# Decoder, second layer: weight loads behind a gather, one layernorm ahead of a softmax step, five weight folds moved into the self-attention

## The chip, the cores and the metric

One core of one Trainium2 chip runs the whole program in one launch. The metric is device time in microseconds (us), the median of several executions. TensorE (PE) multiplies and transposes, VectorE (DVE) and ScalarE (ACT) work on what it leaves in PSUM, GpSimd (POOL) works in SBUF, and SyncE (SP) issues nearly all the loads. Each engine takes its instructions strictly in the order written; semaphores order the engines among themselves.

## The reference

Two pre-norm decoder layers over x of 16 x 64 x 256 floats. The first is a Mamba block, a cross-attention and a routed feed-forward; the second is what the change touches:

```python
x = x + _L0_ffn_ref(_layernorm(x), w_router, w_fc, w_proj)      # two experts, top 1
x = x + _L1_attn_ref(_layernorm(x), Wqkv, b_qkv, Wout, b_out)   # 16 heads of 16, causal, bias by distance
x = x + _L1_xattn_ref(_layernorm(x), ctx, mask, Wq, Wk, Wv, Wo) # 16 heads of 128, 8 key/value heads
x = x + _L1_ffn_ref(_layernorm(x), w_gate, w_up, w_down)        # weights rounded to -1, 0, 1
```

In the second cross-attention the kernel never makes the keys or values: it multiplies Wv by Wo and Wq by Wk once per head ("folds"), and works with the context itself.

## The kernel before

The 1,024 tokens lie as 8 tiles of 128 rows (`x`, `xn`), in four groups g of two tiles. A layernorm of group g is `ln_add` (statistics, DVE), `ln_rstd` (ACT), `ln_scale` (DVE), `ln_turn` (PE transposes) and `ln_turned` (ACT copies to `xnT`). The batches fall into two halves of 512 tokens.

**Feed-forward of layer 0.** Ten sorted jobs; job s leaves its result by `result(s)` (ACT) and a store to `f_out` (SP). POOL's `gather(h)` (L487) fetches the rows of half h back into `xn` with four indirect DMAs, and DVE's `add_back(h)` (L1956) adds them to x. Before it, the same queue writes rows out by indirect DMAs (`scatter`, L485).

**Self-attention of layer 1.** Eight steps i, four heads of one half each; steps 0 to 3 are the first half, 4 to 7 the second. A step is `a_scores(i)` (PE, L1450), `a_shifts(i)` (DVE, L1999: add the bias L2004, row maximum L2008, subtract L2009), `a_exps(i)` (ACT, L828), `a_sums(i)` (DVE, L2015), `a_turn(i)` (PE, L1467), `a_turned(i)` (ACT, L835), `a_context(i)` (PE, L1480). Queries and keys come from `a_project(n)`, n = 0 to 3 for the first half, 4 to 7 for the second (L1426), and from `projected(n)` (ACT). All engines' orders are written out by hand: PE's in L1514 to L1584, ACT's in L851 to L908, DVE's in L2032 to L2096. On DVE the second half's `add_back(1)` and layernorm stand between steps 1 and 2, with `ln_scale(3, 2)` and `ln_scale(3, 3)` behind `a_shifts(2)`. On PE `a_scores(3)` stands ahead of `ln_turn(3, 2)`. On ACT, from step 5 on, `a_exps(i)` stands ahead of `a_turned(i - 1)`. `weight_sum(i)` (L844, ACT) takes the absolute sum of a feed-forward weight. `a_turn_rows` and `a_out` (PE) end a half, and `ln_add(4, g)` follows.

**Loads.** SP issues `wo1` (2,048 KB), `t_gate`, `t_up` and `t_down` (1,024 KB each) as soon as the feed-forward's last `hidden` and `down_rows` are done (L412 to L417).

**Cross-attention of layer 1.** `cross(1, ...)` (L1140 on PE, L664 on ACT) starts with 16 folds, 8 of `wvo` (L1158) and 8 of `wqk` (L1172). Each is one PSUM bank, banks 6 and 7 in turn, emptied by one ACT copy; the last `a_turn_rows(1)` and `a_out(1)` stand after the fourth and the eighth. Then come the first queries (L1184) and eight steps with the scores in L1231. `wvo` and `wqk` lie in region C, where the self-attention's queries, keys, values and softmax tiles lie as well, so no fold can be stored before these are done with.

POOL adds the output bias to all of x in one instruction (L503), and later rounds the three feed-forward weights in 36 instructions (L511 to L515).

## Time and profile before

| | before |
|---|---|
| median of 3 runs | 927.2 us (924.82 to 931.52) |
| the profiled execution | 926.82 us, of which the span of the profile is 924.9 us |
| mean granted clock of TensorE | 0.963 of full speed |
| self-attention, from the last job's result to the first query | 620.4 to 707.0 us of the span |
| cross-attention and feed-forward of layer 1, from the first query | 707.0 us to the end |

The profile is of one execution. All times within the kernel are us from the start of its span. Beside the span, 1.9 us of that execution lie outside it.

### The profile page before, as it was taken

The page shows a single profiled execution, that of the slowest core. Times are in us where ns is not written, and L with a number is a line of the kernel's source. Part 1 is how long each engine was busy: PE and PEld are TensorE (multiplying, and loading weights), DVE is VectorE, ACT ScalarE, POOL GpSimd, SP SyncE. Part 2 cuts the span into 40 slices and gives each one's busy share as a digit, 9 for nine tenths or more (in the row PEclk, how much of TensorE's full clock was granted, in tenths as well). Part 3 has the DMA queues.
Part 4 walks back from the last instruction along what each step waited for, and adds up shares of the span by engine and source line. Part 5 has one row for each costly group of instructions (what it writes and reads, how often), then busy time and mean ns, then how long its engine had stood idle before and what let it go on. Part 6 is the DMA issues. An engine that isn't in the chain of part 4 may idle for free.

```text
span 924.9 us, 12509 instructions
## 1 busy us (share of the span) xinstructions
PE 818.7 (89%) x5082; PEld 501.8 (54%) x5082; DVE 548.1 (59%) x666; ACT 434.1 (47%) x650; POOL 302.3 (33%) x147
## 2 busy tenths in 40 slices
PE   6687797977999889999999899997989799989976
PEld 2232333322445456566666676666677566667754
DVE  3799989899994232333433452437872534464686
ACT  3764666635524555555545312233554222232475
POOL 0089999899870000000001010102009990000000
PEclk9889999899999999999999999998989999999999
DMA  9666666776994100000000031415000000000001
GB/s 301 176 172 172 185 166 172 181 182 181 249 264 157 47 1 1 1 1 1 1 1 25 27 103 57 176 44 226 2 3 1 1 1 1 1 1 1 1 1 46
DMA packets 26377, 77.02 MB, mean 83 GB/s; under 512 B 3569, under 2 KB 10481, under 8 KB 25073
## 3 DMA queue, kind: packets, MB, share of 16 engines
q1 hardware_dynamic: 25552, 74.13, 27.8%
q0 software_dynamic: 768, 2.10, 0.6%
q8 instruction: 41, 0.67, 0.3%
q14 instruction: 16, 0.12, 0.0%
HBM read 68.75 MB, written 7.08 MB: 82 GB/s over the span
## 4 chain that ended last, share of the span: by engine, by line
PE 54%; DVE 13%; DMA 11%; ACT 10%; POOL 6%; issue 5%; SPq 0%; POOLq 0%; DVEq 0%; ACTq 0%
PE ps L1268 11%; PE ps L1184 9%; DMA region_b<-m_rows 5%; DMA region_c<-m_rows 4%; PE ps L1231 4%; PE ps L1367 4%; PE ps L1393 4%; POOL region_c L464 3%; PE ps L1256 3%; PE ps L1189 2%; POOL region_b L464 2%; DVE region_c L1827 2%; PE ps L1073 2%; PE ps L1025 2%; PE ps L1158 2%
## 5 line engine op out<-in xcount | busy, mean ns | idle before, releaser
L464 POOL TENSOR_TENSOR region_c<-region_c,region_b 128x1024 f32<-128x1024 f32 x42 | 101.1, 2415 | 51.6 <-DMA region_b<-m_rows 45.5
L1073 PE MATMUL ps<-region_c,ident 128*128 128x512 f32 x168 | 90.7, 669 | 18.9 <-POOL region_c L464 12.1
L1827 DVE TENSOR_TENSOR_SCAN region_c<-region_c,ps 128x1024 f32<-128x1024 f32 x43 | 97.8, 2283 | 2.0 <-ACT ps L635 0.8
L485 POOL DMA_INDIRECT f_in<-xn,f_row x8 | 8.0, 996 | 275.3 <-DVE f_row L1938 273.5
L1268 PE MATMUL ps<-region_c 128*128 128x256 f32 x384 | 90.4, 381 | 0.1
L1268 PEld LDWEIGHTS ps<-region_c 128*128 128x128 f32 x384 | 72.2, 190 | 24.8 <-issue 16.3
L1904 DVE COPY region_b<-ps 128x512 f32<-128x512 f32 x32 | 21.6, 689 | 84.9 <-PE ps L1242 84.8
L1822 DVE TENSOR_TENSOR ps<-ps,region_c 128x1024 f32<-128x1024 f32 x52 | 63.2, 1215 | 8.7 <-PE ps L1061 8.5
L1073 PEld LDWEIGHTS ps<-region_c,ident 128*128 128x128 f32 x168 | 33.7, 209 | 58.5 <-issue 34.5
L1184 PE MATMUL ps<-xnT,region_a 128*128 128x512 f32 x128 | 61.5, 602 | 0.8 <-ACT region_c L703 0.8
L1184 PE MATMUL ps<-xnT,region_c 128*128 128x512 f32 x128 | 58.6, 594 | 0.7 <-ACT region_c L731 0.7
L464 POOL TENSOR_TENSOR region_b<-region_c 128x1024 f32<-128x1024 f32 x21 | 50.7, 2414 | 8.9 <-DVE region_c L1827 4.0
L629 ACT ACTIVATE region_c<-region_c,a_log 128x1008 f32<-128x1008 f32 x43 | 47.9, 1128 | 9.0 <-DVE region_c L1827 8.7
L695 ACT ACTIVATE region_c<-ps 128x512 f32<-128x512 f32 x32 | 19.1, 597 | 66.7 <-PE ps L1184 66.7
L1827 DVE TENSOR_TENSOR_SCAN region_c<-region_a,ps 128x1024 f32<-128x1024 f32 x21 | 47.9, 2282 | 2.7 <-issue 1.4
L1073 PE MATMUL ps<-region_b,ident 128*128 128x512 f32 x84 | 42.3, 627 | 7.9 <-POOL region_b L464 5.8
L1025 PE MATMUL ps<-xnT,region_b 128*128 128x512 f32 (+1 forms) x96 | 46.6, 619 | 0.7 <-ACT xnT L536 0.7
L698 ACT ACTIVATE region_c<-ps 128x512 f32<-128x512 f32 x32 | 19.1, 597 | 58.4 <-PE ps L1184 58.4
L1061 PE MATMUL ps<-region_b,sel_b 96*128 96x512 bf16 x104 | 32.6, 398 | 14.7 <-DVE region_c L1827 14.7
L1869 DVE TENSOR_TENSOR region_c<-ps,small 128x1024 f32<-128x1024 f32 x8 | 9.8, 1224 | 53.4 <-PE ps L1231 53.4
L731 ACT ACTIVATE region_c<-ps 128x512 f32<-128x512 f32 x48 | 25.3, 599 | 33.3 <-PE ps L1256 33.3
L511 POOL TENSOR_SCALAR region_b<-region_b,small 128x512 f32<-128x512 f32 x12 | 25.0, 2082 | 43.4 <-PE ps L1500 43.4
(246 smaller groups left out, 1640.8 us busy)
## 6 DMA issues: line engine op xcount, KB each, us to landing
region_b<-m_rows SPq DMA_DIRECT2D x43, 512.0 KB, 5.1
region_c<-m_rows SPq DMA_DIRECT2D x21, 512.0 KB, 4.9
xn<-m_brows SPq DMA_DIRECT2D x12, 512.0 KB, 4.4
region_a<-in_x_wo SPq DMA_DIRECT2D x2, 2048.0 KB, 11.5
m_rows<-region_b SPq DMA_DIRECT2D x4, 512.0 KB, 5.7
region_a<-in_x_wq SPq DMA_DIRECT2D x8, 256.0 KB, 7.2
region_b<-in_f_fc SPq DMA_DIRECT2D x1, 2048.0 KB, 7.9
region_b<-in_f_proj SPq DMA_DIRECT2D x1, 2048.0 KB, 13.2
```

Source lines behind the costliest of these rows:

```text
L464: pool.tensor_tensor(m_hc[u % 3], m_h[u % 3], m_cb[u % 3], ALU.mult).then_inc(sem("m_hc"), 1)
L629: act.activation(m_da[u % 3][:, :, 1:S], m_delta[k % 2][:, :, 1:S], ACT.Exp, scale=a_log[:, k, n:n + 1]).then_inc(sem("m_da"), 1)
L1025: last = pe.matmul(ps[0:rows, pair_at + c, :], lhs(k), (rhs if rhs is not None else xnT[:, k, :])[:, c * HALF:c * HALF + HALF], start=(k = ...
L1061: last = pe.matmul(ps[:, 2 * (u % 2) + c, :], sel_b[:, u % 32, :], m_sb[:, u // 32, c * HALF:c * HALF + HALF], start=True, stop=True)
L1073: last = pe.matmul(ps[:, 4 + c, :], ident[:, :], m_hc[u % 3][:, c * HALF:c * HALF + HALF], start=(n == 0), stop=(n == DST - 1))
L1184: last = pe.matmul(b, w, xnT[:, k, cols(it)], start=(k == 0), stop=(k == KH - 1))
L1231: last = pe.matmul(ps[64 * (b % 2):64 * (b % 2) + 64, 4 + a // 2, c:c + S], q_T[:, a, S * b:S * b + S], keys_T[:, S * b:S * b + S], start= ...
L1268: last = pe.matmul(tiles2(2 * (it // 4) + t // 2)[:, t % 2, :], o_Ts[layer][it % 2][:, a, 128 * t:128 * t + 128], wvo[:, 4 * (it % 4) + a, ...
L1367: last = pe.matmul(ps[:, 4 + 2 * (s % 2) + c, :], f_xT[h][:, j, k, :], f_fc[:, bass.ds(weights_at[s] + (HID * k + HALF * c), HALF)], start ...
L1393: last = pe.matmul(ps[:, 2, 0:D], f_aT[s % 2][:, hb, :], f_proj[:, bass.ds(weights_at[s] + D * hb, D)], start=(hb == 0), stop=(hb == HB - 1))
L1822: dve.tensor_tensor(inputs(u), inputs(u), m_du, ALU.mult).then_inc(sem("m_dbu"), 1)
L1827: dve.tensor_tensor_scan(m_h[u % 3], m_da[u % 3].rearrange("p b t -> p (b t)"), inputs(u), 0.0, ALU.mult, ALU.add).then_inc(sem("m_scan"), 1)
```

## The change

- The loads of `wo1`, `t_gate`, `t_up` and `t_down` wait until all eight gathers have landed (`f_back` at 128).
- On DVE `ln_scale(3, 2)` and `(3, 3)` stand ahead of `a_shifts(2)`; on PE `ln_turn(3, 2)` and `(3, 3)` stand ahead of `a_scores(3)`, and `a_turn(2)` behind `a_project(4)` and `(5)`; ACT's order follows, with `a_exps(2)` behind `ln_turned(3, 3)` and `a_turned(2)` behind `projected(5)`.
- On ACT `a_turned(4)` and `a_turned(5)` stand ahead of `a_exps(6)`, and the weight sums are placed anew.
- Five folds (`EARLY`: wqk 0, wvo 0 to 3) are made within the self-attention: one behind `a_context(1)`, four between `a_context(5)` and `a_turn(6)`. Eleven are left in `cross(1, ...)`. For this `wvo` of layer 1 lies over `wo1` and `wqk` over `wqT1` in region A, and feed-forward tiles move to region C.
- `a_turn_rows(1)` still stands after four of the folds that are left and `a_out(1)` after eight; three folds then stand ahead of the first query where there were eight.
- POOL adds the output bias in two halves, the first ahead of `gather(1)`, the second when the last `a_sums` is done.

```diff
             sp.wait_ge(sem("f_h"), JOBS)
-            load(wo1, io["x1_wo"], "ld_x1")
+            sp.wait_ge(sem("f_back"), 128)
+            load(wo1, io["x1_wo"], "ld_t")
             for i, name in enumerate(("t_gate", "t_up")):
                 load(t_w[i], io[name], "ld_t")
...
+            def out_bias(h):
+                pool.wait_ge(sem("ln_xn"), 3 * NT + 4 * (h + 1))
+                pool.tensor_tensor(x[:, 4 * h:4 * h + 4, :], x[:, 4 * h:4 * h + 4, :],
+                                   a_bo.unsqueeze(1).to_broadcast([128, 4, D]), ALU.add).then_inc(sem("a_bo"), 1)
+
             gather(0)
+            pool.wait_ge(sem("ld_a"), 80)
+            out_bias(0)
             gather(1)
-            pool.wait_ge(sem("ld_a"), 80)
-            pool.wait_ge(sem("ln_xn"), 4 * NT)
-            pool.tensor_tensor(x[:, :, :], x[:, :, :], a_bo.unsqueeze(1).to_broadcast([128, NT, D]), ALU.add)\
-                .then_inc(sem("a_bo"), 1)
-            pool.wait_ge(sem("t_ws"), 1)
+            pool.wait_ge(sem("a_den"), 8)
+            out_bias(1)
             pool.wait_ge(sem("x1_mask"), 1)
...
+            def early_folded(m):
+                act.wait_ge(sem("x1_fold"), m + 1)
+                act.activation(fold_out(1, *EARLY[m]), ps[:, 6 + m % 2, :], ACT.Copy).then_inc(sem("x1_folded"), 1)
...
             ln_rstd(3, 2)
             ln_rstd(3, 3)
-            a_exps(2)
+            early_folded(0)
             ln_turned(3, 2)
             ln_turned(3, 3)
-            a_turned(2)
+            a_exps(2)
             projected(4)
             projected(5)
+            a_turned(2)
...
             a_exps(4)
-            for i in range(5, 8 + 1):
+            a_exps(5)
+            a_turned(4)
+            weight_sum(1)
+            a_turned(5)
+            a_rows_turned(0)
+            early_folded(1)
+            early_folded(2)
+            a_exps(6)
+            early_folded(3)
+            early_folded(4)
+            weight_sum(2)
+            for i in range(7, 8 + 1):
...
+            def early_fold(m):
+                what, i = EARLY[m]
+                if m >= 2:
+                    pe.wait_ge(sem("x1_folded"), m - 1)
+                if what == "wvo":
+                    pe.wait_ge(sem("ld_t"), 64)
+                    last = fold_wvo(1, i, ps[:, 6 + m % 2, :])
+                else:
+                    pe.wait_ge(sem("ld_x1"), 48)
+                    last = fold_wqk(i, ps[:, 6 + m % 2, :])
+                last.then_inc(sem("x1_fold"), 1)
...
-            a_scores(3)
+            early_fold(0)
             pe.wait_ge(sem("f_y"), JOBS)
             ln_turn(3, 2)
             ln_turn(3, 3)
-            a_turn(2)
+            a_scores(3)
             a_project(4)
             a_project(5)
+            pe.wait_ge(sem("x1_folded"), 1)
+            a_turn(2)
...
                 a_context(i - 2)
+                if i == 7:
+                    for m in range(1, 5):
+                        early_fold(m)
+                    pe.wait_ge(sem("x1_folded"), 5)
...
             a_sums(0)
-            a_shifts(2)
             ln_scale(3, 2)
             ln_scale(3, 3)
+            a_shifts(2)
             a_sums(1)
```

## Rows read from the trace of the kernel before

**Rows 1.** The page's first two parts: busy time of each engine, granted clock in 40 slices.
```profile
PE 818.7 (89%) x5082; PEld 501.8 (54%) x5082; DVE 548.1 (59%) x666; ACT 434.1 (47%) x650; POOL 302.3 (33%) x147
...
PEclk9889999899999999999999999998989999999999
```

**Rows 2.** Windows of us: busy time by engine, granted clock, DMA share, GB/s.
```profile
627.00:631.00 4.00, 4.00 (x40) 3.03 (x40) 3.93 (x5) 0.90 (x1) 1.35 (x2) 1.00 0.96 399
...
635.00:640.00 5.00, 1.35 (x64) 1.15 (x64) 4.89 (x14) 1.01 (x5) 0.00 (x0) 0.85 0.41 165
670.00:675.00 5.00, 1.63 (x90) 1.50 (x82) 4.93 (x5) 2.79 (x4) 0.00 (x0) 0.77 0.01 3
```

**Rows 3.** The chain of waits, 600 to 740 us: start, length, what.
```profile
627.71 7.00 DMA xn<-f_out,f_row
...
634.74 1.69 DVE x L1959 x4
...
643.06 0.74 DVE xn L1738 x2
```

**Rows 4.** From issue to landing: the indirect writes of L485, then the gathers of L493.
```profile
DMA to landing us min/median/max: 2.4/2.4/2.9
...
DMA to landing us min/median/max: 6.6/7.0/7.5
```

**Rows 5.** DVE's timeline: start, length, instruction; in brackets its idle time before.
```profile
629.98 1.28 DVE L1996 TENSOR_TENSOR region_c<-ps,region_a 128x512 f32<-128x512 f32 x2
...
647.99 2.23 DVE L2009 TENSOR_TENSOR region_c<-region_c 128x1024 f32<-128x1024 f32 x1
...
653.91 1.23 DVE L2004 TENSOR_TENSOR region_c<-ps,region_a 128x1024 f32<-128x1024 f32 x1 [2.56 <-PE ps L1462]
...
660.56 1.23 DVE L2004 TENSOR_TENSOR region_c<-ps,region_a 128x1024 f32<-128x1024 f32 x1 [1.78 <-PE ps L1462]
...
676.87 1.21 DVE L2015 TENSOR_REDUCE region_c<-region_c 128x16 f32<-128x1024 f32 x1
680.68 0.69 DVE L1727 TENSOR_TENSOR x<-ps,x 128x512 f32<-128x512 f32 x1 [2.60 <-PE ps L1510]
```

**Rows 6.** PE's timeline in the self-attention and up to the first query.
```profile
640.68 2.04 PE L1462 MATMUL ps<-region_c 32*64 32x64 f32 x64 [2.65 <-DVE region_c L2004]
...
674.30 1.91 PE L1489 MATMUL ps<-region_c 64*64 64x16 f32 x64 [3.37 <-ACT region_c L835]
...
677.89 4.41 PE L1510 MATMUL ps<-region_b,region_d 128*128 128x256 f32 x16
682.23 1.12 PE L1489 MATMUL ps<-region_c 64*64 64x16 f32 x64
...
687.64 3.79 PE L1158 MATMUL ps<-region_a 128*128 128x256 f32 x16
...
706.89 3.67 PE L1184 MATMUL ps<-xnT,region_c 128*128 128x512 f32 x8
```

**Rows 7.** ACT's timeline: the first weight sum, and the exponentials of step 6.
```profile
658.95 1.90 ACT L848 ACTIVATE region_b<-region_b 128x2048 bf16<-128x2048 f32 x1
...
672.21 1.06 ACT L828 ACTIVATE region_c<-region_c 128x1024 f32<-128x1024 f32 x1 [3.96 <-DVE region_c L2009]
```

**Rows 8.** One line's instructions: ns min/median/max, first and last start.
```profile
L1510 PE MATMUL ps<-region_b,region_d x32: 379/379/631, 677.9 to 698.9; 128*128 128x256 f32 x32
```

**Rows 9.** PE's timeline within the context of step 1.
```profile
637.22 0.81 PE L1489 MATMUL ps<-region_c 64*64 64x16 f32 x42 [1.62 <-issue]
```

**Rows 10.** DMA queues in 634 to 636 us: packets, MB, share of 16 engines.
```profile
q8 instruction: 1, 0.02, 3.4%
```

**Rows 11.** POOL's timeline: the bias, and its last rounding of a weight.
```profile
644.59 4.54 POOL L503 TENSOR_TENSOR x<-x,region_a 128x2048 f32<-128x2048 f32 x1 [15.93 <-DVE xn L1738]
...
762.04 1.50 POOL L515 TENSOR_SCALAR region_b<-region_b 128x512 bf16<-128x512 f32 x1
```

**Rows 12.** DVE's scalings between 640 and 710 us: ns min/median/max.
```profile
L1738 DVE TENSOR_SCALAR xn<-x,mv,rstd x12: 400/406/750, 643.1 to 705.1; 128x256 f32<-128x256 f32 x12
```

More of the change, by code:

```diff
@@ L282, in paired @@
             return int(layer == 0 and it < 7)
+        EARLY = [("wqk", 0), ("wvo", 0), ("wvo", 1), ("wvo", 2), ("wvo", 3)]
+        LATE_WVO, LATE_WQK = range(4, NH // 2), range(1, NH // 2)
         def head_order(layer):
@@ L286, in head_order @@
             if layer == 1:
-                order += [(("wvo", i, 0), "act") for i in range(NH // 2)]
-                order += [(("wqk", i, 0), "act") for i in range(NH // 2)]
+                order += [(("wvo", i, 0), "act") for i in LATE_WVO]
+                order += [(("wqk", i, 0), "act") for i in LATE_WQK]
             for it in range(8 + 1):
@@ L1137, in _, with fold_wvo, fold_wqk @@
                     ln_turn(1, 1)
+            def fold_wvo(layer, i, b):
+                wv_h, wo_h = (wvT, wo) if layer == 0 else (wvT1, wo1)
+                for a in range(2):
+                    h = 2 * i + a
+                    last = pe.matmul(b[:, 256 * a:256 * a + 256], wv_h[:, h if layer == 0 else h // 2, :],
+                                     wo_h[:, h, :], start=True, stop=True)
+                return last
+            def fold_wqk(i, b):
+                for a in range(2):
+                    for k in range(KH):
+                        c = (2 * a + k) * 128
+                        last = pe.matmul(b[:, c:c + 128], wqT1[:, 2 * i + a, 128 * k:128 * k + 128],
+                                         wkT1[:, i, :], start=True, stop=True)
+                return last
             def cross(layer, beside):
@@ L1152, in cross @@
                 filled = sem(tag + "_filled")
[L1153 removed]
                 def fold(i):
[L1155 to L1160 removed]
+                    fold_wvo(layer, i, bank(("wvo", i, 0))).then_inc(filled, 1)
                 if layer == 1:
                     pe.wait_ge(sem("a_pT"), 16)
[L1164 removed]
+                    pe.wait_ge(sem("x1_folded"), len(EARLY))
+                    for i in LATE_WVO:
                         fold(i)
                         beside(-1, f"fold {i}")
[L1167 to L1174 removed]
+                    for i in LATE_WQK:
+                        fold_wqk(i, bank(("wqk", i, 0))).then_inc(filled, 1)
+                        beside(-1, f"wqk {i}")
                 def cols(it):
@@ L1268, in project_out @@
                         last = pe.matmul(tiles2(2 * (it // 4) + t // 2)[:, t % 2, :], o_Ts[layer][it % 2][:, a, 128 * t:128 * t + 128],
[L1269 removed]
+                                         wvo[layer][:, 4 * (it % 4) + a, :], start=(it % 4 == 0 and a == 0 and t % 2 == 0),
                                          stop=(it % 4 == 3 and a == 3), skip_group_check=True)
@@ L1983, in _ @@
                 last = dve.tensor_scalar(qb_half[:, e, :], qkb[:, 0:2], parity[:, e:e + 1], None, ALU.mult)
-            last.then_inc(sem("a_qb"), 1)
+            after(last)
             after(dve.tensor_tensor(g_col, gq_col, gk_col, ALU.mult))
```

74 lines of the change are left out of this document (28 added, 46 removed).

## The prediction

> **What bounds the kernel now.** The page first: PE is busy for 89% of the span and no other engine for more than 59% [rows 1], so from the second quarter on time is won only by taking work off PE's queue or by filling holes in it. The digits of the granted clock show a second thing: in a few slices TensorE is at less than full speed. Then the windows, to see where the holes are. In the self-attention two of five us stand out, 635 to 640 with PE busy for 1.35 us and 670 to 675 with 1.63 us, and in both DVE is busy for 4.9 us or more [rows 2]. So this stretch is bound by DVE and by the order of the queues, while what follows it is bound by PE. In both windows the granted clock falls, and after each hole the first matmuls run at half rate, the 1.2 of the two levels of 1.2 and 2.4 GHz: a context step takes 1.91 us where it takes 1.12 us a little later, and sixteen matmuls of the output projection 4.41 us, 379 ns for each being the normal pace and 631 ns the longest [rows 6, 8].
>
> The chain of waits tells what opened the first hole: the last gather, issued at 627.71 us, lands 7.00 us later, DVE adds it back at 634.74, and through the layernorm the xn for PE's transposes comes at 643.06 [rows 3]. The second hole is 3.37 us ahead of a context, put down to ACT's L835 [rows 6]; ACT in its turn stood in front of the exponentials of step 6 until 672.21 [rows 7], because its queue has `a_exps(6)` ahead of `a_turned(5)`. DVE's timeline gives what DVE itself loses to PE: 2.56 and 1.78 us ahead of two bias additions, waiting for `a_scores(4)` and `(5)`, which stand behind the projections of the second half [rows 5].
>
> **The change part by part.** I walk the three queues PE, ACT and DVE from 620.3 us on in their new order, each instruction with its duration of before at full clock. The same walk in the old order, with the two clock falls put in as seen, brings the first query to 706.2 us against the 706.9 measured [rows 6]; so I use differences.
>
> *Loads behind the gather.* While the gathers run, the DMA engines are busy for 0.96 of the time at 399 GB/s [rows 2], with the loads issued just before them. With nothing beside them, indirect transfers of the same size and through the same queue land after 2.4 us; the gathers took 6.6 to 7.5 us [rows 4]. Alone, the last one would land near 627.71 + 2.4 = 630.1 us. DVE is free at 629.98 + 1.28 = 631.26 us [rows 5] and would begin there, and not at 634.74: **3.5 us**. The writes are the nearest row, not the same transfer, so the bounds are 0 (it takes 7 us by itself) and 3.5 us (DVE is late next), and I take the upper one, since 2.4 leaves 1.1 us to spare. The moved loads are 5,120 KB; at 399 GB/s they take 13 us and land near 645 us. Their first user is ACT's first weight sum, at 658.95 us before [rows 7] and near 652.5 us in the walk, so they are hidden with 7 us to spare. SP has nothing behind them but the final stores.
>
> *ln_scale ahead of a_shifts(2), and PE's order.* On DVE this costs nothing in sum; it delays step 2 by two times some 0.7 us and brings xn earlier by the three instructions of a shift, 3.6 us. In the walk the scaling is at 636.0 us, the transposes at 636.7 and 637.3, the scores of step 3 at 638.6, the two projections at 639.6 to 643.1, and the scores of step 4 at 646.3, which DVE then wants at 646.9. DVE's waits of 2.56 and 1.78 us become 0.4 and 1.6 us: **2.3 us**. The subtraction that took 2.23 us while POOL added the bias (644.59 to 649.13) [rows 5, 11] takes some 1.2 again, since the first half of the bias now comes ahead of `gather(1)`, when DVE waits for the feed-forward's last jobs, and the second half comes later: **1.0 us**. What the walk takes back on the way (exponentials 2 wait a little longer) is 0.3 us. The last sum of step 6 ended at 676.87 + 1.21 = 678.1 us [rows 5] and ends near 671.5.
>
> *ACT's order.* With `a_turned(5)` ahead of `a_exps(6)` the context of step 5 runs directly behind the scores of step 7, at 664 us. The 3.37 us hole is gone, and with it the half rate behind it: the first output projection (4.41 us and not 3.6) and the steps around it lose 2.5 us to the clock before. What is late next is again DVE, which waited 2.60 us for that projection [rows 5] and would wait 0.75. From the end of that sum to the first fold it was 9.6 us (678.1 to 687.64); in the walk it is 7.5 without the bias: **2.1 us**.
>
> *The bias in halves.* The second half is released by the last `a_sums`, just when DVE turns to the scalings of the fourth layernorm, which are on the path. Half of 4.54 us is 2.3 us of POOL [rows 11]. Scalings take 400 ns alone and up to 750 ns beside POOL [rows 12]; four of them: **-0.8 us** with what follows (bounds 0 and -1.4). This is a wait of nobody else: the addition that needs it is 10 us later.
>
> *Five folds.* Four folds of two matmuls take 3.79 us with their pipeline's tail, 0.91 us each at the pace of 16 x 0.228 [rows 6]. Five fewer ahead of the first query: **4.55 us**. What they cost where they go: the first fills PE's time while xn is scaled, 0.1 us at most. The other four (3.6 us) run while PE would wait for the exponentials of step 6; these stand in ACT's queue behind two of the copies and start 2.0 us later than DVE allows, and the transposes of step 6 wait for the last copy. Walked with and without the folds, PE comes out of it 1.1 us later. I have kept that within the terms above (the 2.1 us). If PE were not idle there, all 4.55 us would be given back. Three folds are left between the last output projection and the first query; the layernorm of groups 2 and 3 is needed behind two query products, and in the walk it is ready at 697.0 us and asked for at 697.6, so nothing waits, with 0.6 us to spare.
>
> *Instruction loading.* One of PE's waits is put down to no one: 1.6 us in the middle of a context step [rows 9], up to 637.22, and a packet of PE's instructions moved just then, in 634 to 636 us [rows 10], while the loads still ran. It cost nothing, since DVE was late. The loads now run from 631 to 645 us, where PE crosses two or three such packets and where DVE soon waits for PE. Bounds: 0, and one wait of 1.6 us on the path; the walk with it comes out 0.55 us later. I take 0.3. The Trainium skill ("Runtime: NRT & Kernel Launch", on instruction fetch mechanics) has the next block fetched while the current one executes, the cost mostly hidden; by it this term is 0, and this trace, with its 1.6 us, does not quite agree.
>
> *Sum:* 3.5 + 2.3 + 1.0 - 0.3 + 2.1 - 0.8 + 4.55 - 0.3 = 12.05, say 12 us. Nothing of it is given back later that I can see: the cross-attention behind is PE's own work at full rate, and the rounding on POOL, which starts some 9 us earlier with the same work, ended at 763.5 us [rows 11], eight steps ahead of its user. The profiled execution was 926.8 us (0.4 below the median of 927.2), so it becomes 914.8 and the median **915 us**.
>
> **The rivals.** *A: the clock falls once more.* The new order still leaves holes of 0.7 to 1.2 us around 637 to 645 us. In the trace the clock fell at the holes of 1.62 and 2.65 us and at that of 3.37 us [rows 2, 6, 9]; of several near 1 us one after another these rows don't tell. The walk with half rate from 638 to 648 us comes out 4.2 us later: gain 8, 919 us. *B: the gather takes 7 us by itself*, because reading rows from memory is slower than writing them. For it: all eight took 6.6 to 7.5 us [rows 4]; against it: both fours ran beside heavy loads. It gives up 3.5 us and risks the clock for 1.2: gain 7.5 to 8.5, 919. *C: the gaps close but the time comes back*, that is, the work filled in is not in a hole: if PE and DVE hand each other the same lateness at each step, only the gather is won and some of the folds, gain 4 to 6, 922. It needs the walk to be wrong, which the old order speaks against. *D: slower.* The moved loads land too late: ACT's first weight sum waits for all four of them and stands ahead of `a_exps(4)`, so every us behind 652.5 delays DVE, PE and all after them one for one. To eat 12 us they must land at 664.5, that is 5.24 MB in 33 us, 160 GB/s; the loads made 399 [rows 2]. Landing at 668 gives 931 us. *E: more than forecast.* If the holes that remain shrink too, or later falls of the clock shift away, another 2 to 3 us: 912.
>
> **How the numbers follow.** Forecast 0.52, A 0.13, B 0.10, C 0.13, D 0.04, E 0.08. The likeliest case alone reaches from 913 to 917.5 us. The range must take in A, B and E: 911 to 921. A change of 1% is 9.3 us, about what a measurement of this kernel can tell, so faster by over 1% means below 917.9: the forecast nearly whole, E, and a third of A and B, 0.68. Within 1%: the rest of A and B, and C, 0.28. Slower: D, 0.04.
>
> **What would show it.** In the changed profile: the last gather landing 2.4 to 3 us after its issue; `add_back(1)` at 631.3 us behind DVE's own work and not behind the DMA; the bias addition of step 4 waiting 0.4 us and not 2.56; no hole of 3 us at the context of step 5 and full clock from 665 to 680 us; four fold instructions there; the first query near 694 us; and from there to the end the same 218 us. I am wrong if the clock is at half anywhere between 635 and 690, if ACT's L848 waits for a DMA, or if the stretch behind the first query has changed by over 2 us.

## The result: 5.8 us gained, half of what was forecast

The changed kernel takes 923.1 us (median of 8 runs, 919.05 to 925.67), the kernel before 930.2 us beside it (8 runs, 924.82 to 933.08): ratio 0.9937, 95% interval 0.991 to 0.9963, that is 5.8 us (3.4 to 8.4) less. Forecast were 12 us, from 927.2 to 915, with a range of 911 to 921; 923.1 lies outside it. The profiled execution took 924.2 us, its span 922.3.

The total alone hides where it went, because the time up to the last job's result, which the change doesn't touch, differed between the profiles of this study, from 618.4 to 626.0 us. So all profiles are read in two pieces: the **stretch** from the last job's result on ACT to the first query product on PE (forecast: 73.6 us by the first query near 694, 74.5 by the sum of 12.05), and **behind**, from there to the end. Before they are 86.5 and 218.0 us; after 82.0 (624.80 to 706.80) and 215.5. The stretch gave 4.5 us and not 12, and "behind" gave 2.5 where nothing was forecast.

The page after, first and second part, answers to [rows 1]:

```profile
PE 822.4 (89%) x5082; PEld 502.2 (54%) x5082; DVE 549.7 (60%) x666; ACT 433.7 (47%) x650; POOL 302.3 (33%) x148
...
PEclk9889899899899999999999999999999999999999
```

Windows after (us; busy time and count of PE, PE's weight loads, DVE, ACT and POOL; granted clock, DMA share, GB/s), against [rows 2]. The first and the third lie as far behind the last result (14.6 and 49.6 us) as the two windows of before do:

```profile
639.43:644.43 5.00, 2.83 (x74) 2.70 (x75) 4.93 (x8) 0.90 (x6) 0.00 (x0) 0.92 0.97 408
643.00:647.00 4.00, 4.00 (x54) 3.67 (x58) 3.42 (x3) 2.15 (x4) 0.00 (x0) 0.58 1.02 424
674.43:679.43 5.00, 4.21 (x24) 3.25 (x23) 4.93 (x5) 4.67 (x6) 0.00 (x0) 1.00 0.01 2
```

The second hole is filled: PE is busy for 4.21 us of five, where it was 1.63. The first is filled only in part, 2.83 us where it was 1.35. And between 643 and 647 us the granted clock is 0.58, and there the DMA engines are busy throughout. PE's timeline after, against [rows 6, 9], says how the clock fell there, and once more at 688 us:

```profile
639.52 0.53 PE L1518 MATMUL ps<-region_c 64*64 64x16 f32 x22 [0.74 <-ACT region_c L850]
642.13 0.81 PE L1518 MATMUL ps<-region_c 64*64 64x16 f32 x42 [2.08 <-issue]
642.88 1.43 PE L1174 MATMUL ps<-region_a 128*128 128x128 f32 x8
644.10 1.92 PE L1030 MATMUL ps<-ident,xn 128*128 128x128 f32 x8
...
673.33 3.81 PE L1166 MATMUL ps<-region_a 128*128 128x256 f32 x16
...
688.33 1.97 PE L1030 MATMUL ps<-ident,xn 128*128 128x128 f32 x8 [1.86 <-DVE xn L1785]
690.09 0.43 PE L1736 MATMUL ps<-small,ones 128*128 128x3 f32 x2
690.38 5.89 PE L1166 MATMUL ps<-region_a 128*128 128x256 f32 x16
```

The context of step 1 (L1518) stops behind its 22nd matmul for 2.08 us, put down to no one: it is the same place in the same step as the 1.62 us of [rows 9], 42 matmuls from the end. Then the transposes of xn (L1030) take 1.92 us at half rate. At 688.33 transposes take 1.97 us and the first four folds 5.89 us, behind a wait of 1.86 us for DVE's scaling; the four early folds at 673.33 took 3.81. DVE's timeline after, against [rows 5, 12]:

```profile
630.78 1.23 DVE L2051 TENSOR_TENSOR region_c<-ps,region_a 128x1024 f32<-128x1024 f32 x1 [1.01 <-PE ps L1491]
...
635.63 1.66 DVE L2006 SCALAR_TENSOR_TENSOR x<-xn,small,x 128x256 f32<-128x256 f32 x4
...
640.31 1.37 DVE L1785 TENSOR_SCALAR xn<-x,mv,rstd 128x256 f32<-128x256 f32 x4
...
647.69 1.22 DVE L2051 TENSOR_TENSOR region_c<-ps,region_a 128x1024 f32<-128x1024 f32 x1 [1.23 <-PE ps L1491]
...
655.33 1.22 DVE L2051 TENSOR_TENSOR region_c<-ps,region_a 128x1024 f32<-128x1024 f32 x1 [2.77 <-PE ps L1491]
...
680.86 0.69 DVE L1774 TENSOR_TENSOR x<-ps,x 128x512 f32<-128x512 f32 x1 [1.35 <-PE ps L1551]
...
685.75 3.17 DVE L1785 TENSOR_SCALAR xn<-x,mv,rstd 128x256 f32<-128x256 f32 x4 [0.37 <-ACT rstd L540]
```

`add_back(1)` (L2006) starts directly behind DVE's own work, 10.8 us after the result, where it was 14.4 behind the DMA. But the additions of steps 3 and 4 (L2051) wait 1.23 and 2.77 us for scores that the stop and the half clock made late; for step 4 a wait of 0.4 was forecast. And the four scalings at 685.75 take 3.17 us where the same four took 1.37 at 640.31. POOL's timeline after, against [rows 11], has the second half of the bias beside them:

```profile
685.46 2.34 POOL L505 TENSOR_TENSOR x<-x,region_a 128x1024 f32<-128x1024 f32 x1 [52.37 <-DVE region_c L2062]
```

One of the four took 2205 ns and the other three 400 each (that line's instructions, min/median/max 400/400/2205): the first stood from 685.75 until 0.15 us behind the end of POOL's instruction at 687.80.

### The profile page after: what moved, and what is told of

Same layout as the page of the kernel before. It is cut to its first block, busy times and chain, and to the rows that moved or that the text cites. A ratio compares the mean times of both kernels' runs of the same rounds, so it can differ in the third digit from the quotient of the medians.

```text
span 922.3 us, 12515 instructions
## 1 busy us (share of the span) xinstructions
PE 822.4 (89%) x5082; PEld 502.2 (54%) x5082; DVE 549.7 (60%) x666; ACT 433.7 (47%) x650; POOL 302.3 (33%) x148
## 4 chain that ended last, share of the span: by engine, by line
PE 56%; ACT 11%; DVE 11%; DMA 9%; POOL 7%; issue 6%; SPq 0%; POOLq 0%; DVEq 0%; ACTq 0%
PE ps L1297 11%; PE ps L1213 9%; DMA region_b<-m_rows 5%; POOL region_c L468 4%; PE ps L1396 4%; PE ps L1422 4%; PE ps L1285 4%; PE ps L1260 4%; DMA region_c<-m_rows 3%; PE ps L1218 2%; PE ps L1095 2%; PE ps L1047 2%; POOL region_b L468 2%; PE ps L1166 2%; PE ps L1465 2%
## 5 line engine op out<-in xcount | busy, mean ns | idle before, releaser
L1213 PE MATMUL ps<-xnT,region_a 128*128 128x512 f32 x256 | 120.1, 599 | 1.4 <-ACT region_c L718 0.8
L1213 PEld LDWEIGHTS ps<-xnT,region_a 128*128 128x128 f32 x256 | 47.2, 190 | 41.2 <-issue 35.8
L1297 PE MATMUL ps<-region_c 128*128 128x256 f32 x256 | 59.8, 380 | 0.0
L1297 PEld LDWEIGHTS ps<-region_c 128*128 128x128 f32 x256 | 48.5, 190 | 16.7 <-issue 11.5
L1095 PE MATMUL ps<-region_b,ident 128*128 128x512 f32 x84 | 44.7, 658 | 8.1 <-POOL region_b L468 6.0
L1285 PE MATMUL ps<-region_b,ctxn 64*128 64x256 f32 x256 | 38.4, 433 | 3.7 <-ACT region_c L746 2.5
## 6 DMA issues: line engine op xcount, KB each, us to landing
region_a<-in_x_wo SPq DMA_DIRECT2D x2, 2048.0 KB, 10.9
```

The lines of the kernel that those rows point to most:

```text
L1095: last = pe.matmul(ps[:, 4 + c, :], ident[:, :], m_hc[u % 3][:, c * HALF:c * HALF + HALF], start=(n == 0), stop=(n == DST - 1))
L1213: last = pe.matmul(b, w, xnT[:, k, cols(it)], start=(k == 0), stop=(k == KH - 1))
L1285: last = pe.matmul(banks[r].rearrange("p (s a q) -> p s a q", s=2, a=4)[:, s], ctxn[64 * r:64 * r + 64, 4 * (it // 4) + 2 * m + s, :], mov ...
L1297: last = pe.matmul(tiles2(2 * (it // 4) + t // 2)[:, t % 2, :], o_Ts[layer][it % 2][:, a, 128 * t:128 * t + 128], wvo[layer][:, 4 * (it % ...
```

## The experiments

Theory 1: PE's stop is a fetch of instructions that stands in line with the loads, and it costs the clock. Theory 2: the second half of the bias costs far more than 0.8 us, since DVE's scaling is on the path. The rival of both: the time comes back whatever is done there. Each ratio is to runs of the kernel before taken beside it on the same chip; stretch and behind are read from one profiled execution of each kernel.

| kernel | stretch | behind | median us | ratio (95%) |
|---|---|---|---|---|
| e1_bias_later | 78.3 | 215.9 | 917.0 | 0.9874 (0.9848 to 0.9901) |
| e2_loads_later | 78.3 | 215.5 | 920.9 | 0.9932 (0.9897 to 0.9967) |
| e3_both_later | 73.8 | 216.0 | 916.4 | 0.9886 (0.9857 to 0.9914) |
| e4_loads_as_before | 77.7 | 216.1 | 918.4 | 0.9895 (0.9861 to 0.9929) |
| e6_bias_later_again | 80.6 | 216.0 | 920.3 | 0.993 (0.9911 to 0.9949) |
| e7_both_later_again | 80.6 | 216.0 | 921.4 | 0.9941 (0.9916 to 0.9966) |
| e8_eight_more_products | 82.3 | 215.5 | 923.7, one run | |
| e5_no_early_folds | 84.4 | 218.5 | 927.5 | 0.9994 (0.9977 to 1.0011) |
| e9_only_loads_behind | 83.9 | 219.5 | 927.6 | 0.9993 (0.9973 to 1.0013) |
| e10_act_order_as_before | 86.4 | 217.1 | 925.8 | 0.9993 (0.9971 to 1.0015) |
| e11_before_again | 86.4 | 218.0 | 925.7, one run | |
| e12_after_again | 85.2 | 215.9 | 923.5, one run | |
| e13_gather_held | 80.4 | 217.6 | 921.1 | 0.9931 (0.9903 to 0.996) |
| e14_bias_later_third | 80.7 | 216.8 | 923.2 | 0.9918 (0.9888 to 0.9948) |
| e15_scores_1_early | 77.7 | 216.8 | 918.1 | 0.9889 (0.9859 to 0.9918) |
| e16_scores_1_and_loads | 73.4 | 217.6 | 913.5 | 0.9847 (0.9813 to 0.988) |

### The two costs, one at a time and together

e1_bias_later: the second half of the bias waits for the attention's division, a step behind the scalings.

```diff
-            pool.wait_ge(sem("a_den"), 8)
+            pool.wait_ge(sem("a_o"), 4)
             out_bias(1)
```

> The changed kernel with one edit: the second half of the output bias on POOL is released by the end of the second division on DVE (a_o at 4) and not by the last sum. In the changed kernel the four scalings of the fourth layernorm took 3.17 us beside it, PE sat idle for 1.86 us and its clock fell until about 695 us. Theory (POOL's addition blocks these scalings, and the clock falls because of that hole): the four scalings take 1.4 us, the hole is under 0.3 us, the sixteen matmuls of four folds take 3.8 and not 5.9 us, and the stretch from the last job's result to the first query falls from 82.2 to 77 or 78 us. Rival (the scalings wait for something else, or the clock falls anyway): the stretch stays within 1 us of 82.2.

e2_loads_later: the four loads wait until the context of step 1 is done.

```diff
-            sp.wait_ge(sem("f_back"), 128)
+            sp.wait_ge(sem("a_ctx"), 2)
             load(wo1, io["x1_wo"], "ld_t")
```

> The changed kernel with one edit: the four weight loads wait for the context of step 1 (a_ctx at 2) and not for the gathers. In the changed kernel, as in the one before, PE stopped in the middle of that context, at its 22nd instruction, for 2.1 us (1.6 before) with no engine to wait for, while the loads ran, and its clock fell behind it. Theory (a fetch of PE's instructions waits in the DMA engines behind the loads): the stop is gone, the clock holds around 644 us, DVE waits under 1.2 us for the scores of step 4 where it waited 2.77, and the stretch falls from 82.2 to 78.5 to 80 us. Rival (PE outruns its fetches with the DMA engines idle too): a stop of 1.5 us or more stays at the same instruction, and the stretch stays near 82.

e3_both_later has both edits.

> Both edits at once. If both theories hold the stretch is 74 to 76 us and the kernel is 6 to 8 us faster than the changed one, 13 to 14 faster than the one before. If only that of the bias holds 77 to 78 us; if only that of the fetch holds 78.5 to 80 us.

e4_loads_as_before has e1's edit and the loads where they were before the change.

```diff
-            sp.wait_ge(sem("f_back"), 128)
             load(wo1, io["x1_wo"], "ld_t")
```

> As the first of these four (the bias later), and the loads where they were in the kernel before, beside the gathers. Theory (the gathers take 7 us because of the loads, and alone 2.5 to 3): the last gather lands 3.5 us later against the end of DVE's work on the values, and the stretch is 3 to 4 us longer than in the run with the bias alone. Rival (the stop in the context hides this gather anyway, since PE is stopped for 2 us in both): under 1.5 us longer.

DVE's timeline of e1_bias_later:

```profile
686.43 1.38 DVE L1785 TENSOR_SCALAR xn<-x,mv,rstd 128x256 f32<-128x256 f32 x4 [0.36 <-ACT rstd L540]
```

and PE's, of the same kernel:

```profile
687.22 1.31 PE L1030 MATMUL ps<-ident,xn 128*128 128x128 f32 x8
688.36 0.28 PE L1736 MATMUL ps<-small,ones 128*128 128x3 f32 x2
688.50 3.79 PE L1166 MATMUL ps<-region_a 128*128 128x256 f32 x16
```

The scalings are back at 1.38 us, PE doesn't wait, the folds take 3.79 us. The stretch is 3.7 us shorter (82.0 to 78.3); with the loads later in both it is 4.5 (78.3 to 73.8). The 3.7 is too small a price, since e1's stop in the context of step 1 happened to be longer (2.36 us against 2.08). From the end of the last sum of step 6, ahead of the bias, to the first query it is 27.3 us in after, 26.0 in e2 and 27.1 in e12 (after once more, below), and 22.6 in e1, e3 and in the other kernels below that are after with the bias later and no fold moved: the second half of the bias cost 3.4 to 4.7 us. Some 1.8 us of it is the scaling itself (3.17 less 1.38), the rest the half clock. The medians confirm it: the ratio goes from 0.9937 to 0.9874, with intervals that don't meet.

PE's timeline of e2_loads_later, in the context of step 1:

```profile
633.12 1.12 PE L1518 MATMUL ps<-region_c 64*64 64x16 f32 x64 [0.74 <-ACT region_c L850]
634.17 1.16 PE L1174 MATMUL ps<-region_a 128*128 128x128 f32 x8
635.17 1.04 PE L1030 MATMUL ps<-ident,xn 128*128 128x128 f32 x8
```

No stop, and full rate. The stretch is 3.7 us shorter than after's, and 4.5 shorter from e1 to e3. e4_loads_as_before shows the other side: there the stop was 2.44 us, and the stretch (77.7) is that of e1 (78.3), as its rival had it. With the stop in place, loading behind the gathers bought nothing.

When the packet of instructions moves says how the stop hangs on the loads. The DMA queues of after in 639.5 to 640.0 us (packets, MB, share of 16 engines), 14.7 to 15.2 us behind the last result:

```profile
q1 hardware_dynamic: 13, 0.21, 99.3%
q8 instruction: 1, 0.02, 11.8%
```

and of e3 in 630.0 to 630.5 us, 11.2 to 11.7 behind it:

```profile
q8 instruction: 1, 0.02, 11.7%
```

In e3, where nothing else moves at that time, the packet starts some 3.5 us earlier than in after, where it moves among the loads. PE is at its 22nd matmul 15.2 us behind the result in both, and in after goes on at 17.3 us. In e1 the packet starts in 15.0 to 15.5 us and PE goes on at 17.6; in e2 the packet ahead of the context of step 1 is not late and nothing stops there. e2 has a smaller stop of the same kind further on, where its own loads run:

```profile
646.02 0.46 PE L1491 MATMUL ps<-region_c 32*64 32x64 f32 x12 [0.88 <-issue]
```

In the packet records of the trace PE goes on 1.3 to 1.5 us behind the end of a packet in all six of these stops (before, after, e1, e2, e4, e15). So the packet comes late beside the loads and PE waits for it. That PE's instructions are what this queue carries is inferred, from this order and from PE's being the engine with by far the most instructions.

The price of the stop has a weaker support than that of the bias. The executions profiled of e2 and e3 (914.09 and 910.42 us) were the fastest of their seven and six, and the ratios show no gain from the later loads alone: 0.9932 against 0.9937, and 0.9886 against 0.9874. What supports it in the whole is the last pair below, e15 and e16.

e3_both_later has both cured: 12.7 us of the stretch are won (86.5 to 73.8), where the terms of the sum without these two costs make 13.15. Forecast was a stretch of 74 to 76 us.

### The same kernels again, and a third wait

The next four kernels, on another chip, didn't come out alike. e6_bias_later_again is e1 and e7_both_later_again is e3, unchanged. e8_eight_more_products is e1 with eight of the score products of step 2 made twice, so that all later instructions of PE lie further on in its stream.

```diff
                                                 a_k[rows, g // 2, S * b:S * b + S], start=True, stop=True)
+                                if i == 2 and j < 1:
+                                    last = pe.matmul(ps[64 * s:64 * s + 64, 4 + a, c:c + S],
+                                                     a_qh[e][rows, g // 2, S * b:S * b + S],
+                                                     a_k[rows, g // 2, S * b:S * b + S], start=True, stop=True)
```

> The kernel with the bias later once more, beside the one with both edits on the same chip. In the first runs the profiled stretches were 78.3 and 73.8 us, but the medians of the whole (917.0 and 916.4 us) did not show that difference; the time up to the last job's result differs by up to 6 us from one execution to another. Expected: stretch 78 to 79 us, a stop of 2 to 2.5 us in the context of step 1.

> If the loads behind the context of step 1 are worth what the profile says, this is 3 to 5 us faster in the median than its neighbour with the bias alone, and its profiled stretch is 73.5 to 75 us again. Rival (only that profiled execution was spared): the stop comes back in the profile, or the medians are within 1 us of each other.

> The kernel with the bias later, and eight products of the scores of step 2 made twice (the same values to the same place; sixteen more matmuls in the records, each with its weight load, ahead of the context of step 1). Theory (PE's instructions come in blocks of fixed length, and the stop is the wait for the next block): the stop in the context of step 1 moves sixteen matmuls forward in the work, from behind the 22nd to behind the 6th, give or take one. Rival (the stop belongs to the data or to the time since the loads began): it stays behind the 22nd, or is gone.

e5_no_early_folds is e3 with all 16 folds in the cross-attention, as before the change.

```diff
-        EARLY = [("wqk", 0), ("wvo", 0), ("wvo", 1), ("wvo", 2), ("wvo", 3)]
+        EARLY = []
```

> Both edits, and all sixteen folds in the cross-attention again; all other orders as in the changed kernel. Theory (five folds of 0.91 us run in time that PE would have waited, all but 1.1 us): the stretch is 3 to 4 us longer than the 73.8 us with both edits. Rival (they only change places): within 1 us of it.

On this chip e6 and e7 have the same stretch, 80.6 us, and medians 1.1 us apart: loading later gains nothing, and both expectations missed. DVE's timeline of e6_bias_later_again says what is late instead:

```profile
630.13 1.23 DVE L2051 TENSOR_TENSOR region_c<-ps,region_a 128x1024 f32<-128x1024 f32 x1 [4.00 <-remote]
```

and PE's, the contexts of steps 0 and 1:

```profile
635.98 1.91 PE L1518 MATMUL ps<-region_c 64*64 64x16 f32 x64 [1.86 <-ACT region_c L850]
...
640.48 1.91 PE L1518 MATMUL ps<-region_c 64*64 64x16 f32 x64 [0.69 <-ACT region_c L850]
```

DVE waits 4.00 us ahead of the addition of step 1, 3 us more than the 1.01 in after's profile above, and the releaser is none that the trace knows ("remote"). PE then waits 1.86 us and runs at half rate for some 10 us (windows of e6 and of e3, from 12.8 and 15.2 us behind their last results, same columns as above):

```profile
634.00:646.00 12.00, 9.45 (x160) 8.55 (x152) 10.69 (x23) 5.09 (x11) 0.00 (x0) 0.58 0.95 399
```

```profile
634.00:646.00 12.00, 10.85 (x273) 8.23 (x268) 11.33 (x14) 6.96 (x12) 0.00 (x0) 1.00 0.85 337
```

Behind the last result the context of step 0 came at 14.8 us where e1 has 11.8, and that of step 1 at 19.3 where e1 has 14.7, whole and with no stop, though the loads ran beside it. The packet of instructions started in 636.5 to 637.0 us, 15.3 to 15.8 behind the result, as late as in e1, but now ahead of PE. So e8 has no stop to shift and told nothing on its question.

PE itself was slower already ahead of DVE's wait. The scores of step 1 and the values behind them in e6,

```profile
625.83 1.66 PE L1491 MATMUL ps<-region_c 32*64 32x64 f32 x64
627.42 4.54 PE L1475 MATMUL ps<-region_b,xnT 128*64 128x256 f32 x32
```

and in e1:

```profile
629.19 1.28 PE L1491 MATMUL ps<-region_c 32*64 32x64 f32 x64
630.40 3.73 PE L1475 MATMUL ps<-region_b,xnT 128*64 128x256 f32 x32
```

That makes 1.2 us, at full granted clock in both. And the semaphore that these scores raise for DVE goes up, in the updates that the trace records, within 0.03 us of their last matmul in e1 and 2.6 us behind it in e6, in both just ahead of DVE's start. By this record it is the signal that comes late; DVE isn't held.

e5 against e7, both with the long wait: the five early folds are worth 3.8 us of the stretch (84.4 to 80.6) and 2.5 us behind it, and 6.1 us in the medians (927.5 to 921.4).

### Is the wait in the kernel before too, and what makes it

e9_only_loads_behind is the kernel before with the one wait added:

```diff
             sp.wait_ge(sem("f_h"), JOBS)
+            sp.wait_ge(sem("f_back"), 128)
             load(wo1, io["x1_wo"], "ld_x1")
```

> The kernel before with one edit of the change: the four loads wait for the gathers. Theory (alone the gather lands early enough for DVE to go straight from the values to the adding back): the DVE idle time of 3.47 us ahead of it is under 0.3 us; DVE's work of the stretch comes 3.2 to 3.5 us earlier, but the stop in the context of step 1 stays (1.5 to 2.5 us), and DVE is not late enough to hide it all: the stretch is 83 to 85 us against 86.5. Rival (the stop eats the whole): 86 or more.

e10_act_order_as_before is e3 with the old order on ACT:

```diff
+            a_exps(6)
             a_turned(5)
             a_rows_turned(0)
             early_folded(1)
             early_folded(2)
-            a_exps(6)
```

> Both edits of the better version, and on ACT the exponentials of step 6 ahead of the copies of step 5, as in the kernel before. Theory (the copies of step 5 then wait for DVE's step 6): the context of step 5 waits some 3 us, its clock may fall behind it, and the stretch is 2 to 4 us longer than 73.8. Rival (exponentials 6 come 2 us earlier and pay for it): within 1 us.

e9 has the wait (3.96 us), and so has e10; e9's stop is gone with it. The moved loads alone give 2.6 us of the stretch in the profile and nothing in the whole (0.9993): a gain that the total doesn't confirm. e10 is 5.8 us longer than e7, more than the 2 to 4 expected (86.4 against 80.6; another chip, the same wait), and PE's timeline has the hole of [rows 6] back, 3.37 us and half rate behind it:

```profile
673.83 1.91 PE L1518 MATMUL ps<-region_c 64*64 64x16 f32 x64 [3.37 <-ACT region_c L850]
```

e11_before_again and e12_after_again are the two kernels as they stand. e13_gather_held is e1 with the gather of the second half held back until the scores of step 1 are done, e14_bias_later_third is e1 beside it.

```diff
+            pool.wait_ge(sem("a_s"), 2)
             gather(1)
             pool.wait_ge(sem("a_o"), 4)
```

> The kernel before, unchanged, profiled beside the next three. If the wait of 4.00 us ahead of the addition of step 1 belongs to the chip or the execution and not to the edits, it is here too, or in none of the four; the stretch is 86.5 us without it, 88 to 91 with it.

> The changed kernel, unchanged. Stretch 82.0 us without the wait of 4.00 us; with it 84 to 86 (80.6 with the bias later, and 3.7 to 5 us for the bias beside the scalings).

> The kernel with the bias later, and POOL issues the second gather only when the scores of step 1 are done (a_s at 2), so nothing of the gather is under way at that time. Theory (the gathers being issued or moved delay DVE's release): no idle time over 1.1 us ahead of the addition of step 1 whatever the chip; the gather lands 3 us later, so where the next run has the wait the stretch is within 1.5 us of it, and where it has not, 2 to 4 us longer. Rival (the wait has nothing to do with the gather): the 4.00 us are here if they are in the next run.

> The kernel with the bias later, for comparison on this chip: stretch 80.6 us with the wait of 4.00 us, 78.3 without.

DVE's timeline of e11_before_again, the unchanged kernel before:

```profile
628.33 1.22 DVE L2004 TENSOR_TENSOR region_c<-ps,region_a 128x1024 f32<-128x1024 f32 x1 [4.06 <-remote]
```

DVE's of e13_gather_held:

```profile
624.27 1.23 DVE L2052 TENSOR_TENSOR region_c<-ps,region_a 128x1024 f32<-128x1024 f32 x1 [0.96 <-PE ps L1492]
...
632.49 1.67 DVE L2007 SCALAR_TENSOR_TENSOR x<-xn,small,x 128x256 f32<-128x256 f32 x4 [3.28 <-DMA xn<-f_out,f_row]
```

and POOL's of the same kernel:

```profile
629.14 0.95 POOL L497 DMA_INDIRECT xn<-f_out,f_row  x1 [0.30 <-issue]
```

So the wait doesn't come from the change. It is in all nine profiles on the chips numbered 12 and 8 whose kernel issues the gather ahead of the scores' use, the kernel before among them, and in none of the four on chip 0, nor in the two recorded first. Each is one execution, so it goes with the chip as far as these profiles show; whether single executions on a chip differ in it is not shown. In all nine PE's scores and values are as slow as in e6 and the signal is as late. The wait ends 0.7 us behind POOL's fourth indirect issue, and with these issues held back it is 0.96 us. Before the change it cost nothing, since DVE waited for the gather anyway (stretch 86.4 with it, 86.5 without, where 88 to 91 was expected); after it, it takes back 3 us: e12 has 85.2 where the recorded profile has 82.0. Holding the gather is no cure, because it lands later: 80.4 us and 80.7.

The gather with no loads beside it took 632.49 - 629.14 = 3.35 us from issue to use, where 2.4 was estimated and 7.0 was seen beside the loads. For all four gathers of e1, again with no loads beside them, the view of POOL's L497 has:

```profile
DMA to landing us min/median/max: 2.7/2.7/3.5
```

### A version that is faster than both

e15_scores_1_early is e1 with the scores of step 1 ahead of `a_project(3)`, so that DVE has them before POOL's issues; e16_scores_1_and_loads is e3 with the same.

```diff
             a_project(2)
-            a_project(3)
             a_scores(1)
+            a_project(3)
```

> The kernel with the bias later, and on PE the scores of step 1 between the two projections behind step 0 and not behind them, so that they are done about 3.9 us behind the last job's result, when POOL has just begun to issue the gathers (2.9 us). Theory A (a release by PE is late only while the gathers are issued): no wait of 4 us; DVE goes straight from step 0 to step 1, add_back begins 10.8 us behind the result and not 13.8, and the stretch on a chip with the wait falls from 80.6 to 76 to 78.5 us (the stop in the context of step 1 may come back). Theory B (DVE's start is held while the gathers are issued): DVE still waits until 9.0 us behind the result, and the stretch stays at 80 to 81.

> The same with the loads behind the context of step 1. Under theory A the stop in that context is gone too, and the stretch is 73.5 to 75 us, 12 us less than before (86.4), on any chip; the kernel is 11 to 15 us faster than the one before. Under theory B 80 to 81.

e15 has the stretch (77.7 us) and the early `add_back(1)` (10.4 us behind the result) of theory A, and the stop is there again. PE's timeline of e15:

```profile
640.70 0.81 PE L1518 MATMUL ps<-region_c 64*64 64x16 f32 x42 [2.43 <-issue]
```

DVE's timeline of e16:

```profile
626.11 1.22 DVE L2051 TENSOR_TENSOR region_c<-ps,region_a 128x1024 f32<-128x1024 f32 x1
```

No wait at all, neither of 4 us nor of 1, and in the window 634 to 646 us:

```profile
634.00:646.00 12.00, 10.38 (x212) 7.66 (x207) 11.79 (x19) 7.49 (x15) 0.00 (x0) 1.00 0.65 251
```

In e16 no stop is left. Its median is 913.5 us (911.31 to 918.27), ratio 0.9847: 14.2 us under the kernel before by its own ratio, and its stretch is 0.4 us off e3's. From e15 to e16, which differ in the loads alone, the stretch is 4.3 us shorter and the median 4.5 us, though the intervals of the ratios overlap a little: here the whole agrees with the stop's price. These two ran on chip 6, and no kernel with the old order of scores ran there. That the early scores remove the long wait is therefore not shown, only that it is absent.

## Where the prediction was right and where it was wrong

The gain was forecast as 12 us with a range of 6 to 16 around it; 5.8 came. Two terms failed, instruction loading and the bias in halves: both were put at a fraction of a microsecond and cost about 4 us each, because behind each the clock fell. Two of its own signs of being wrong came true: half clock between 635 and 690 us, and a change of over 2 us behind the first query. By its own steps:

- **The gather, 3.5 us: held.** `add_back(1)` moved from 14.4 to 10.8 us behind the result. Its working was a little off (2.7 to 3.5 us by itself and not 2.4), with no effect, as DVE is late next. Rival B is excluded. But this term stands only where the long wait doesn't: in e12 `add_back(1)` starts 13.9 us behind the result.
- **Instruction loading, 0.3 us: this step failed.** The prediction said that PE would meet such a stop where DVE soon waits for PE, bounded it by one wait of 1.6 us, and took 0.3. It was 2.08 us in one place, and what the bound left out is the clock: behind the stop the granted clock is 0.58 from 643 to 647 us, and the waits of 1.23 and 2.77 us follow. The price in the stretch is 3.6 to 4.5 us (in after; e3 against e1; e16 against e15), more than twice the outer bound. Rival A had this mechanism, at 4.2 us for the clock, with a chance of 0.13; it named small holes as the opener and not the stop. The Trainium skill ("Runtime: NRT & Kernel Launch", on instruction fetch mechanics) has the next block fetched meanwhile and the cost mostly hidden. Here a stop of 2.08 us stands beside DMA engines busy for 0.97 of the time, and is gone where the loads come later; the measurement decides. That it is the fetch rests on its place, on its going with the loads, and on the packet of the instruction queue, which starts some 3.5 us later beside them and just ahead of PE's going on; where blocks end was not shown, since e8 had no stop.
- **The bias in halves, -0.8 us: this step failed in its size, by a factor of four to six.** It measured 3.4 to 4.7 us (from the last sum of step 6 on, after, e2 and e12 against the kernels with the bias later). The prediction took the slowest scaling of [rows 12], 750 ns, as the rate beside POOL. That one ran beside a POOL instruction with one tensor read (L511 to L515). Beside the addition of two tensors DVE's scaling doesn't slow down, it stands until POOL is done, 2205 ns. The nearer row was shown, and used two paragraphs earlier for another purpose: DVE's subtraction of 2.23 us from 647.99 ends 1.09 us behind the 649.13 at which POOL's addition ends [rows 5, 11], its own time being 1.23. The Trainium skill ("SBUF — State Buffer", section "SBUF: two separate sides") has it so: the pair of ports that DVE and GpSimd share is held for a whole instruction and the loser waits. These two rows agree. By that rule the term would have been the rest of POOL's 2.3 us, and the clock that fell behind PE's wait of 1.86 us makes it the 4.7 of after. The scalings of [rows 12] don't agree with the rule: the four at 704 to 706 us ran beside POOL's L511, an instruction with one tensor read, and took 400 to 750 ns.
- **DVE's waits, 2.3 us, and the subtraction, 1.0 us:** with the stop cured they came. In e3 DVE waits 0.54 and 1.78 us ahead of steps 4 and 5 where 0.4 and 1.6 were forecast, and its subtractions take 1.23 us. In after itself the wait of step 4 is 2.77 us, by the stop.
- **ACT's order, 2.1 us: the mechanism held, the size was 1.2.** The hole of 3.37 us and the half rate behind it are gone. From the last sum of step 6 to the first fold behind the projection it was 9.6 us, was forecast as 7.5, and is 8.3 in e3: DVE waits 1.36 us for the projection and not 0.75. The 5.8 us of e10 (against e7, across chips) are not this term alone, since there the four early folds stand behind the hole, at half rate (5.45 us), and no longer in it.
- **Five folds, 4.55 us less 1.1 inside the walk: held.** 3.8 us against 3.5 (e5 against e7; 0.8 of it lies ahead of the last sum of step 6, where the clock is at half for 17 us in e5 and 10 in e7).
- **The loads in time: held.** The first weight sum starts at 660.36 us behind DVE's and ACT's own work and waits for no DMA; rival D is excluded.
- **"Behind" unchanged: wrong, by 2.5 us for the better.** PE's timeline of the kernel before, behind its first softmax of the cross-attention:

```profile
727.72 1.97 PE L1242 MATMUL ps<-ident,region_c 128*128 128x128 f32 x8 [3.02 <-DVE region_c L1896]
```

and of the kernel after:

```profile
727.17 1.09 PE L1271 MATMUL ps<-ident,region_c 128*128 128x128 f32 x8 [2.56 <-DVE region_c L1943]
```

The wait is 3.02 us and then half rate, or 2.56 and full rate: in after the clock holds. The windows of before, the same columns as above,

```profile
707.00:820.00 113.00, 104.33 (x747) 68.48 (x747) 50.28 (x61) 32.79 (x57) 54.98 (x29) 0.98 0.00 1
820.00:925.00 105.00, 89.25 (x560) 62.96 (x558) 70.02 (x128) 51.02 (x66) 0.00 (x0) 0.95 0.03 11
```

and of after,

```profile
707.00:820.00 113.00, 104.24 (x750) 68.13 (x750) 53.65 (x66) 33.62 (x61) 59.59 (x31) 1.00 0.00 1
820.00:922.30 102.30, 86.54 (x555) 60.95 (x553) 68.62 (x127) 50.94 (x65) 0.00 (x0) 0.97 0.03 11
```

say the same for all of it: 0.98 and 0.95 became 1.00 and 0.97. e5 and e9, with no early folds, have 218.5 and 219.5 us behind and the wait of 3.02 us, so the shorter wait goes with the early folds; why it does was not tested. Whether the clock then holds is not steady: e13 and e16 have the wait of 2.56 us too, but half rate behind it (1.97 us), and 217.6 us behind.

**The sum.** The stretch in three pieces, us:

| | before | forecast | after | e3, both cured |
|---|---|---|---|---|
| last result to the end of the last sum of step 6 | 57.7 | 51.1 | 54.7 | 51.1 |
| from there to the first fold behind the projection | 9.6 | 7.5 | 10.9 | 8.3 |
| from there to the first query | 19.2 | 14.7 | 16.4 | 14.3 |

The forecast's column is without its costs of 0.8 and 0.3 us. The pieces end in these rows, of DVE and PE in e3,

```profile
668.74 1.21 DVE L2062 TENSOR_REDUCE region_c<-region_c 128x16 f32<-128x1024 f32 x1
678.27 3.79 PE L1166 MATMUL ps<-region_a 128*128 128x256 f32 x16
```

and of DVE in after:

```profile
678.29 1.21 DVE L2062 TENSOR_REDUCE region_c<-region_c 128x16 f32<-128x1024 f32 x1
```

With both costs cured 12.7 us are won, and the walk of the queues was right nearly piece by piece. In after the stop takes 3.6 us in the first piece and the bias 4.7 in the other two, and 4.5 are left, which with 2.5 behind are 7.0 in the recorded profiles. Where the long wait is, e11 to e12, it is 1.2 + 2.1 = 3.3 us. The measured 5.8 (3.4 to 8.4) lies between. Rival C had this number, 4 to 6 us, but not the reason: it needed the walk to be wrong. The range failed since it held each of these costs apart, at its small size, and not two falls of the clock at once.

**What stays open.** Why one chip has the 4 us wait and another hasn't; what POOL's four issues have to do with PE's slower matmuls and its late signal; whether the early scores cure it; and why the medians on chip 0 don't show the stop's price.

## What to carry to other kernels

A stop of an engine that "cost nothing" belongs to the sum at its full length as soon as the change removes what hid it, and on PE with the half-rate time that follows; here the stop, and on two chips the long wait, were in the kernel before under a wait for the gather. What POOL's addition does to DVE was in a row of before too. Before an instruction of POOL that reads two tensors is moved, look at what DVE has at that moment: in the forms that stood here, price it at the rest of POOL's instruction, not at a slower rate. And read a change by the stretch it touches, since the 600 us ahead of it moved by over 7 us from one execution to the next, more than the change was worth.

## What the hardware showed that was not expected

- PE stopped for 1.62 to 2.44 us at one matmul of the context of step 1 in five profiles (before, after, e1, e4, e15), all with loads beside it (in after at a DMA share of 0.97). It didn't in e2, e3 and e16, where they had not begun, nor in e13, where the packet of instructions moved ahead of them, nor where PE came to that matmul over 3 us later, behind the packet, as in e6.
- A DVE scaling of 400 ns took 2205 (2210 in e12) beside POOL's addition of two tensors, whose end it met within 0.15 us; beside POOL's instructions with one tensor the longest was 750 ns in before [rows 12] and 770 in after. Beside the addition in before, DVE's reductions and its addition with an input in PSUM kept their 1.21 to 1.22 us; its subtraction, both inputs in SBUF, took 2.23.
- On two chips DVE's release for step 1 came some 3 us late (3.96 to 4.1 us of wait against 1.01) while POOL issued four indirect DMAs, in the same program that shows 1.0 elsewhere, and PE's scores took 1.66 us for 1.28.
- A gather of 128 rows of 1 KB took 2.7 to 3.5 us from issue to landing with no loads beside it (e1), and 6.6 to 7.5 us beside the loads [rows 4].
